# Order of the two value subtractions and the last rotary sum on VectorE, in a fused attention and FFN kernel

## What is computed

```python
q = apply_rotary(pos, proj(Wq, bq) * scale)          # (2, 16, 1024, 128)
k = apply_rotary(pos, proj(Wk, bk))
v = proj(Wv, bv)
sim = jnp.where(causal, -big, einsum('bhid,bhjd->bhij', q, k))
out = einsum('bhij,bhjd->bhid', softmax(sim), v)
x = x + ga * (out.transpose(0, 2, 1, 3).reshape(b, n, INNER) @ Wo + bo)
# apply_rotary(pos, t) = t * cos(pos) + rotate_half(t) * sin(pos)
```

## Time and profile before

| | |
|---|---|
| median of 3 runs | 1076.97 us (1075.44 to 1078.8) |
| profiled execution | 1076.11 us |
| its span, first to last instruction | 1074.3 us |
| TensorE busy | 1030.7 us (96%) |
| VectorE busy | 811.6 us (76%) |
| ScalarE busy | 671.5 us (63%) |
| GpSimd busy | 621.2 us (58%) |
| mean granted TensorE clock | 0.989 |

### The profile page before, as it was taken

The page is one execution under the profiler, slowest core; times in us unless marked ns, Lnnn a source line. Parts: engine busy times, 40 slices in busy tenths (PEclk is TensorE's granted clock), DMA queues, the critical chain, the costliest instruction groups (busy, mean ns, idle before and its releaser), DMA issues.

```text
span 1074.3 us, 20576 instructions
## 1 busy us (share of the span) xinstructions
PE 1030.7 (96%) x6368; PEld 919.1 (86%) x6368; DVE 811.6 (76%) x1707; ACT 671.5 (63%) x1443; POOL 621.2 (58%) x473
## 2 busy tenths in 40 slices
PE   6889999999999999999999999999999999988898
PEld 5779898898999899989998998989998999866676
DVE  6857777777777777777788777777777787779665
ACT  5466666666666666666666666666666666646642
POOL 2255755566566656665557555665666565656543
PEclk9889999999999999999999999999999999999899
DMA  9212111221112211221121112211122111410001
GB/s 290 70 32 68 40 41 40 69 49 33 36 38 61 49 39 40 69 49 37 33 66 42 39 39 69 49 34 35 39 60 49 39 40 40 141 40 1 12 30 40
DMA packets 41685, 55.99 MB, mean 52 GB/s; under 512 B 5204, under 2 KB 24724, under 8 KB 41620
## 3 DMA queue, kind: packets, MB, share of 16 engines
q1 hardware_dynamic: 41620, 55.30, 19.9%
HBM read 19.63 MB, written 2.10 MB: 20 GB/s over the span
## 4 chain that ended last, share of the span: by engine, by line
PE 78%; DVE 7%; POOL 5%; issue 4%; DMA 2%; ACT 2%; SPq 1%; DVEq 0%; ACTq 0%
PE ps_r L1182 15%; PE ps_r L1180 15%; PE ps_r L1181 15%; PE ps_t L1301 10%; PE ps_s L1182 5%; PE ps_s L1181 5%; PE ps_s L1180 5%; DMA swapped<-straight 2%; PE ps_s L1187 2%; POOL straight L564 2%; PE ps_s L1190 2%; POOL w_lo L556 2%; POOL swapped L563 2%; PE ps_r L1187 1%; PE ps_r L1189 1%
## 5 line engine op out<-in xcount | busy, mean ns | idle before, releaser
L563 POOL TENSOR_TENSOR swapped<-swapped,sin_sb 128x512 f32<-128x512 f32 x124 | 165.5, 1334 | 244.6 <-DMA swapped<-straight 244.6
L762 ACT ACTIVATE pT_hi<-ps_t 128x512 fp32r<-128x512 f32 (+3 forms) x384 | 186.5, 491 | 94.4 <-PE ps_t L1301 92.4
L1029 DVE TENSOR_TENSOR pT_lo<-ps_t,pT_hi 128x512 fp32r<-128x512 f32 (+3 forms) x384 | 201.7, 549 | 48.3 <-ACT pT_hi L762 48.0
L1056 DVE CUSTOM_DVE_ANT_0 ps_s<-ps_s,mask_wide 128x128 f32<-128x128 f32 (+7 forms) x256 | 194.4, 759 | 56.5 <-PE ps_s L1182 43.7
L570 POOL TENSOR_TENSOR qk_lo<-straight,qk_hi 128x512 fp32r<-128x512 f32 x124 | 159.0, 1292 | 120.8 <-ACT qk_hi L686 120.8
L773 ACT ACTIVATE probs<-ps_s,neg_max 128x128 f32<-128x128 f32 (+7 forms) x256 | 189.9, 742 | 33.0 <-DVE neg_max L1056 29.9
L1301 PE MATMUL ps_t<-ident,probs 128*128 128x128 f32 x1152 | 186.1, 275 | 9.1 <-DVE pT_lo L1029 9.1
L564 POOL TENSOR_TENSOR straight<-straight,cos_sb 128x512 f32<-128x512 f32 x124 | 179.9, 1451 | 0.0
L954 DVE TENSOR_TENSOR straight<-straight,swapped 128x512 f32<-128x512 f32 x126 | 132.0, 1048 | 38.2 <-POOL straight L564 38.1
L1301 PEld LDWEIGHTS ps_t<-ident,probs 128*128 128x128 f32 x1152 | 134.9, 140 | 13.5 <-issue 9.9
L1180 PE MATMUL ps_s<-qk_hi 128*128 128x512 f32 (+3 forms) x384 | 139.3, 363 | 0.5 <-ACT probs L773 0.4
(11 more groups left out here) (179 smaller groups left out, 2259.1 us busy)
## 6 DMA issues: line engine op xcount, KB each, us to landing
swapped<-straight SPq DMA_DIRECT2D x252, 128.0 KB, 2.3
x_in<-in_L_attn_x SPq DMA_DIRECT2D x4, 512.0 KB, 5.8
w_raw<-in_L_attn_Wk SPq DMA_DIRECT2D x8, 256.0 KB, 2.8
w_raw<-in_L_attn_Wq SPq DMA_DIRECT2D x8, 256.0 KB, 3.1
w_raw<-in_L_attn_Wv SPq DMA_DIRECT2D x8, 256.0 KB, 3.5
wo_all<-in_L_attn_Wo SPq DMA_DIRECT2D x1, 2048.0 KB, 11.4
wo_raw<-in_L_attn_Wo SPq DMA_DIRECT2D x8, 256.0 KB, 2.6
x<-in_L_attn_x SPq DMA_DIRECT2D x4, 512.0 KB, 4.2
```

The lines of the kernel that those rows point to most:

```text
L563: pool.tensor_tensor(swapped[:, q, :], swapped[:, q, :], sin_sb[:, cs], ALU.mult)
L762: nc.scalar.activation(turned_at(ORDER[step], k0, k1)(pT_hi), ps_t[:, (T_FIRST[step] + j) % 2, 0:(k1 - k0) * P].rearrange("p (k q) -> p k ...
L1029: nc.vector.tensor_tensor(turned_at(t, k0, k1)(pT_lo), ps_t[:, (T_FIRST[step] + j) % 2, 0:(k1 - k0) * P].rearrange("p (k q) -> p k q", q=P ...
L1056: nc.vector.tensor_tensor_reduce(rows, rows, mask_wide[:, SEQ - n_keys:SEQ], -1.0, -MASKED, ALU.add, ALU.min, accum_out=neg_max[:, t:t + 1 ...
```

## The change

In VectorE's string the subtraction of the second V piece is moved ahead of the sum of Q1. The sum and the subtraction themselves, and the other three strings, stay.

```diff
 VECTOR_PLAN = """max:0 turn:6.0- turn:7.0- turn:7.1- max:1 low:P0- add:K0+ max:2 turn:0.0 add:Q0+ low:P1- max:3
         sum:W00- turn:1.0 max:4 sum:W01- turn:1.1 turn:2.0 sum:W10- max:5 turn:3.0 sum:W11- add:K1+ turn:3.1
-        turn:4.0 max:6 low:V0 add:Q1+ low:V1 max:7 turn:5.0 turn:5.1"""
+        turn:4.0 max:6 low:V0 low:V1 add:Q1+ max:7 turn:5.0 turn:5.1"""
```

## The result

The changed kernel took 1068.14 us (median of 6, 1067.9 to 1070.45) against 1076.26 us (median of 6) before on the same chip: ratio 0.9928, 95% interval 0.9916 to 0.9941. Run again later, with more runs of the kernel before beside it, it gave 0.9941 (0.9925 to 0.9956). The forecast was 1070.3 us, a gain of 6.2; the two ratios give 7.7 and 6.3 us (the medians themselves differ by 8.1 and 5.4).

The account below looks back on a forecast made before the run. TensorE bounds the kernel (78% of the chain), losing time where it stands still, partly for VectorE's value subtraction. Gains 4.9 + 0.6 + 0.7 = 6.2 us brought 1076.5 to 1070.3 us; range 1067.5 to 1073.3.

Parts of the forecast that it names:

- Where the gain lies: TensorE's stops before `make:Q0+` in units 2, 3, 6, 10, 14, 18, 22, 26, and one wait in unit 0.
- The term of the late units: Units 2, 6, 10 to 26, before `make:Q0+`: each stop shrinks by 0.7 us, 4.9 in all, ends 2.8 and 7.8.
- What is late next: In late units the transposes before the long product wait for `exp:7`, behind `out:K0+`: TensorE still stands 0.4 us.
- Unit 3: Its wait of 0.3 us means a stop of 0.6, all gained, as `exp:7` is not late there; ends 0.3 and 0.6.
- Unit 0: TensorE's 0.70 us wait ahead of `make:K0+` at 73.79 goes: gain 0.7 us, ends 0.5 and 0.8.
- Ordinary units: 21 units and unit 0: the sum comes later on VectorE but just in time for `high:Q1+`; cost 0.
- the second cover: On ScalarE in ordinary units, `out:K0+` waits 0.67 us for TensorE, which can absorb a late `high:Q1+`.
- The rule against the trace: The sum's end hangs on the end of GpSimd's subtraction, so starting 0.2 to 0.3 us later doesn't move it.
- rival B: VectorE and GpSimd share speed, so five sums end 0.2 to 0.3 us later: gain 5.0 us, 1071.5; chance 0.08.
- Rival A: `exp:7` does not hold TensorE in late units, so the whole stop goes: gain 9.2 us, 1067.3; chance 0.12.
- Rival C: `exp:7` or a later operation of the next unit holds TensorE: 3.2 us or less gained, about 1073.7; chance 0.11.
- Rival D: Slower: input of `low:V1` late on VectorE in 21 ordinary units, wait over 1.2 us; 1096 at 2 us each; chance 0.03.

Follow-up runs that it names:

- late_units: The kernel before with the new VectorE order only in units 2, 6, 10 to 26, the old one elsewhere: ratio 0.9959.
- other_units: The kernel before with the new VectorE order in all units but 0 and 2, 6, 10 to 26: ratio 0.9997.
- unit0_only: The kernel before with the new VectorE order in unit 0 alone: ratio 0.999.
- after_highv_late: The changed kernel with `high:V1` moved behind `turn:5.0` and `exp:6` in ScalarE's string: ratio 1.0131 against the kernel before.

## Why the prediction was right

*Where the gain lies.* Right. `late_units` has 4.87 us of it, `other_units` 0.3. *The term of the late units*, 7 x 0.7 = 4.9: 5.0 in the first profile, of which some 0.2 is that three units changed from the first kind to the second and one the other way. *What is late next*: right in place and size. The prediction worked it out on a unit of the first kind: `exp:7` 2.99 us after `make:K0+`, the way 4.4 us, the sum starting and ending as before. Unit 18 shows just that: `exp:7` at 3.00 (585.75 - 582.75), the way 4.41, the sum at 0.09 for 1.76. In units of the second kind `exp:7` begins at 2.91 and the way is 4.33; and moving `exp:7-` ahead of `out:K0+` takes most of the rest away. Only the label was foretold wrongly: the stop shows as "issue" on the weight loads, not as "<-ACT probs".

*Unit 3*, 0.6: 0.5 in the first profile, but that is not a fixed size: with the old order its way was 4.52 us before, 4.37 in `late_units` and 4.13 in `unit0_only`, with the new one 3.93 to 4.04. *Unit 0*, 0.7: the wait is gone, its size isn't resolved. *Ordinary units*, 0: right, with the sum at 0.68 as taken, and `high:Q1+` 0.03 later in unit 13, where `out:K0+` stayed at 1.85 us after `make:K0+`: the second cover took it up.

*The rule against the trace.* In unit 6 the sum began 0.98 us after the start of `low:V0` before, and in the changed kernel 1.20 after it; it took 1.77 and 1.55, so it ended 2.75 after it both times, 0.54 and 0.56 behind the end of GpSimd's subtraction. Shared speed (rival B) would have made the end move. Unit 2 against unit 26 above shows it from both sides. It agrees with the rule of the Trainium skill ("SBUF — State Buffer", section "Who interferes with whom") that VectorE, when it has two SBUF inputs, and GpSimd, when it reads SBUF, contend for a port that is an exclusive lock, held for the whole instruction by whichever issues first.

*Rival A*, all comes back: against it stand 4.32 to 4.41 us, not 3.93. *Rival C*, a new wait in the next unit: none, since ordinary units stayed at 28.24. *Rival D* needs a wait of over 1.2 us for the input of `low:V1`; it was 0.15 in unit 13, and `after_highv_late` made it 1.66 there and got the sign.

*The size.* The sum was 6.2 us against 7.7 and 6.3 measured. No step failed; the difference to the first comparison lies in the two stretches outside the loop, which take several us more or less from run to run. The close match of the second total is partly luck, as the total scatters by more than the 0.1 us between them; the loop and its units are what bears the forecast out. The range held it by 0.6 us at its low end.

## What to carry to other kernels

In an in-order queue put first what is ready and is waited for by the bottleneck, but look at what the displaced instruction holds up in turn: here two instructions, `out:K0+` and `max:7`, stood between the gain and the engine, and in the late units `out:K0+` kept 0.3 us of it and `max:7` another 0.1 to 0.2. Ask also who made the operand late. One move in GpSimd's string took the same stop away at its root, while the too simple form of that move only brought another buffer's release late.

When a loop repeats, measure it between two like instructions far apart: the loop scattered by 0.7 us at most here and the way in late units of one kind by 0.03, where the totals of the kernel before scattered by 3.9 to 5.7.

## What the runs showed of the hardware

Which of VectorE's sum and GpSimd's subtraction starts first is worth some 1 us on a 0.68 us instruction: 0.74 us where the sum starts 0.16 ahead, 1.76 where it starts 0.07 behind and 1.55 where it starts 0.29 behind. An instruction that is moved back can become longer, not only later. The value subtraction, with one operand in PSUM, was never touched by it (675 to 691 ns; 673 to 692 in the changed kernel).

TensorE's lower clock level came over 60 to 68 us in eight of the 13 profiles and in the other five not at all, though it is the same part of the program. It doesn't set the length of that stretch by itself: with the same mean granted clock of 0.95 the way up to the loop took 70.14 us in `unit0_only` and 73.88 in `other_units`, TensorE being idle for 14.9 and 18.1 us of it. Over all the profiles that way took 70.1 to 75.1 us: 5 us of the total that no order in the loop explains.
